# Taking out the landing waits inside the second expert layer's token scatter

## The reference, cut to what matters

```python
logits = flat.astype(jnp.float32) @ router_w.T + router_bias
scores = jax.nn.softmax(logits, axis=-1)
topk_scores, topk_idx = jax.lax.top_k(scores, TOPK)
topk_scores = topk_scores / jnp.clip(topk_scores.sum(axis=-1, keepdims=True), 1e-12, None)
h = jax.nn.silu(jnp.einsum('nd,ehd->neh', flat, gate_w)) * jnp.einsum('nd,ehd->neh', flat, up_w)
expert_out = jnp.einsum('neh,edh->ned', h, down_w)
sel = jnp.take_along_axis(expert_out, topk_idx[:, :, None], axis=1)
out = (sel * topk_scores.astype(flat.dtype)[:, :, None]).sum(axis=1)
out = out + jax.nn.silu(flat @ sgate_w.T) * (flat @ sup_w.T) @ sdown_w.T
```

## Time and profile before

| | |
|---|---|
| three runs | 1621.0, 1626.23, 1638.97 us; median 1626.23 us |
| the profiled execution | 1626.23 us, its span 1624.5 us, so 1.7 us lie around it |
| PE busy | 1368.0 us (84% of the span) |
| DVE, ACT, POOL busy | 774.4 us, 438.9 us, 295.9 us |
| scatters of stage 7 | 1265.4 to 1368.6 us in the span |

### The profile page before, as it was taken

How to read it: one execution, slowest core, us unless ns; L and a number is a source line. 1 busy time by engine, 2 the same in 40 slices (tenths; PEclk the granted TensorE clock), 3 DMA queues, 4 the chain that set the end, 5 groups by cost and what they waited for, 6 DMA issues and landing times.

```text
span 1624.5 us, 18832 instructions
## 1 busy us (share of the span) xinstructions
PE 1368.0 (84%) x6042; PEld 767.9 (47%) x6043; DVE 774.4 (48%) x2121; ACT 438.9 (27%) x840; POOL 295.9 (18%) x310
## 2 busy tenths in 40 slices
PE   5999999999934779999998829999957689898983
PEld 3434334333413434444443525666645445677862
DVE  7282383275277435545565422222256563344546
ACT  2122122222105224544353302333222211232320
POOL 2010010010011100000000030111111454145560
PEclk9899999999977769999998859999976579999997
DMA  9999990000001000000000391111024622244436
GB/s 313 338 336 327 335 315 5 0 0 0 0 5 48 1 1 1 1 1 1 1 29 1 108 358 33 33 33 33 23 75 156 232 85 95 82 135 152 144 122 261
DMA packets 136659, 171.35 MB, mean 105 GB/s; under 512 B 8464, under 2 KB 124944, under 8 KB 136464
## 3 DMA queue, kind: packets, MB, share of 16 engines
q1 hardware_dynamic: 126992, 143.81, 28.6%
q0 software_dynamic: 9600, 26.65, 4.5%
HBM read 68.11 MB, written 102.32 MB: 105 GB/s over the span
## 4 chain that ended last, share of the span: by engine, by line
PE 69%; DVE 15%; issue 5%; ACT 4%; SPq 4%; DMA 2%; another core or an unknown queue 1%; POOL 0%; DVEq 0%; ACTq 0%; POOLq 0%
PE psum L1819 16%; PE psum L1204 5%; PE psum L1188 5%; PE psum L1987 5%; PE psum L992 4%; PE psum L880 3%; PE psum L2043 3%; PE psum L1009 2%; PE psum L1776 2%; DVE arena L2558 2%; PE psum L2020 2%; PE psum L1973 2%; PE psum L2067 2%; PE psum L890 2%; SPq L2664 2%
## 5 line engine op out<-in xcount | busy, mean ns | idle before, releaser
L1819 PE MATMUL psum<-arena 128*128 128x512 f32 (+1 forms) x576 | 291.8, 635 | 0.3
L1819 PEld LDWEIGHTS psum<-arena 128*128 128x128 f32 (+1 forms) x576 | 96.5, 192 | 162.8 <-issue 160.0
L2558 DVE TENSOR_REDUCE arena<-psum 128x4 f32<-128x616 f32 x128 | 102.1, 797 | 126.9 <-PE psum L1987 125.6
L1987 PE MATMUL psum<-arena 32*128 32x308 f32 x512 | 112.0, 516 | 24.2 <-DVE arena L2558 22.9
L1132 POOL DMA_INDIRECT ys<-xnT,arena x96 | 92.2, 961 | 122.4 <-DVE xnT L1098 97.5
L2153 ACT ACTIVATE arena<-psum,arena 128x512 f32<-128x512 f32 x72 | 49.1, 686 | 234.2 <-PE psum L1819 222.2
L2267 ACT ACTIVATE arena<-psum 128x2048 f32<-128x2048 f32 x40 | 75.0, 1875 | 76.8 <-PE psum L2024 59.8
L992 PE MATMUL psum<-arena,xn 128*128 x384 | 89.9, 388 | 2.0 <-ACT xn L1043 0.9
L1204 PE MATMUL psum<-arena,xn 128*128 x384 | 88.6, 385 | 2.0 <-ACT xn L1250 2.0
L1188 PE MATMUL psum<-arena,side 128*128 x192 | 88.1, 602 | 1.0 <-ACT side L1243 0.6
L1987 PEld LDWEIGHTS psum<-arena 32*128 32x128 f32 x512 | 41.9, 200 | 92.1 <-DVE arena L2558 61.3
(11 more groups left out here) (391 smaller groups left out, 2220.3 us busy)
## 6 DMA issues: line engine op xcount, KB each, us to landing
xs<-zeros SPq DMA_DIRECT2D x8, 8576.0 KB, 59.8
arena<-in_W SPq DMA_DIRECT2D x16, 1024.0 KB
xn<-xs SPq DMA_DIRECT2D x96, 134.0 KB
arena<-in_gate_up SPq DMA_DIRECT2D x4, 2048.0 KB
arena<-ys SPq DMA_DIRECT2D x4, 2048.0 KB, 15.0
arena<-in_down SPq DMA_DIRECT2D x4, 1024.0 KB
xs<-zeros SPq DMA_DIRECT2D x1, 3120.0 KB, 17.0
side<-xs SPq DMA_DIRECT2D x24, 130.0 KB
```

The lines of the kernel that those rows point to most:

```text
L1819: ins = pe.matmul(bank[dict(hn=4, r=5, z=6, xn=7)[k]][:], lhs[:, cols], r, start=(start and n == 0), stop=(stop and n == len(w) - 1))
L1987: ins = pe.matmul(bank[4 + i][:, 0:2 * M].rearrange("p (h m) -> p h m", h=2), qhT[rows, n % 3, c, t * P:(t + 1) * P], keys[rows, l, c, b, ...
L2558: dve.tensor_reduce(neg[:, n % 2, t, 2 * pair:2 * pair + 2, 2 * c:2 * c + 2], psum[:, 4:6, 0:2 * M].rearrange("p b (h m) -> p b h m", h=2) ...
```

## The change

The wait of L870 and L871 is deleted. Before, POOL held back after the first, second and third tile of each group until every scatter started so far had landed; now it starts the 16 scatters of a group one behind another. The wait for `slots_ready` at the start of each group stays, and so does SP's wait for all 64. Everything behind in the file moves up by two lines.

```diff
@@ -867,8 +867,6 @@
                 for k in range(K4):
                     pool.indirect_dma_start(xs7, bass.IndirectOffsetOnAxis(r7["slot_i"][:, n, k:k + 1].bitcast(U32), 0),
                                             xn[:, g, t], None).then_inc(scattered.sem, 16)
-                if t < GT - 1:
-                    pool.wait_ge(*scattered.at(7, 16 * K4 * (n + 1)))
 
```

## The result

| | before | after |
|---|---|---|
| median | 1626.49 us (20 runs) | 1650.28 us (20 runs) |
| range of the runs | 1617.84 to 1641.11 | 1639.44 to 1668.39 |
| the profiled execution | 1626.23 us, span 1624.5 | 1653.95 us, span 1652.2 |

The changed kernel takes 1.0126 times as long, with a 95% interval of 1.0097 to 1.0155: some 20 us more where no change was forecast. The time lies outside the range.

The account below looks back on a forecast made before the run. PE, with 69% of the chain, was taken to bound the kernel, POOL holding 0%. POOL's 22.4 us and SP's 9.9 us stay hidden, so 1626.23 + 0 = 1626.2 us, range 1616 to 1638.

Parts of the forecast that it names:

- POOL's side: POOL's scatter issue: 22.4 us of waits go, 12.3 us of new waits for DVE's L701 come, last issue ends 9.9 us earlier.
- PE's step into the first quad: PE passing from L890 to L985: still without idle time, near 1391.5 as before, 0 us gained.
- SP's wait at the last weights: SP after its eight token loads: waiting for PE grows from 3.2 to 13.1 us, last weights still at 1382.37.
- POOL's gain: Removed scatter waits: 22.4 us less on POOL, 9.9 us less up to SP, 0 us on PE.
- Two costs have to be asked for, since the same scatters now stand denser: DMA queue and DVE speed beside denser scatters: DMA 0 to some us inside the 9.9, taken as 0; DVE 0.
- The term of the sum that was put at zero: The change's effect on the whole time: 0 us, the 9.9 us hidden by PE's products L880 and L890.
- all it did before that was the shared expert, which takes nothing from the scatters: PE before L985: its work doesn't depend on the scatters, so it arrives at 1391.48 as before.
- Stage 5 shows this very case: Stage 5's 16 scatters without waits, beside transfers filling the DMA engines to 0.97: 961 ns an issue, nothing piled up.
- L697 and L931 at their usual durations: DVE instructions beside scatters and without: 419 to 420 and 686 to 689 ns, so engines don't slow each other by 1%.
- 0 on both sides: Cost of DVE and POOL working beside each other: bounded at 0 us.
- The jam: POOL's 64 starts: its queue fills and starts slow; 1675.5 us if all went at 2.51 us a scatter; chance 0.03.
- What would show it: Trace signs: starts end near 1358.7, L948 near 1361.2, L985 near 1391.5; PE pausing or issues well over 1.0 us refute.

Follow-up runs that it names:

- e6_eights: Changed kernel with landing waits put back after the second and fourth tile of each group, at most eight starts in a row: 1633.00 us, 1.0015.
- e11_twelve: Changed kernel with landing waits put back after the third and fourth tile of each group, runs of twelve and four: 1635.06 us, 1.0023.
- e14_rows: Changed kernel with each indirect scatter sent to 128 consecutive rows, the experts' part of the result left out: 1641.85 us, one run.
- e3_half: Changed kernel with one landing wait put back in each group, after its second tile: 1636.01 us, 1.0054.

## Why the prediction was wrong, point by point

**What held.** POOL's side came as worked out: the pace of 1.27 us, 20.0 us for a group, twelve waits gone, waits for L701 in their place. PE's step into the first quad has no idle time in front of it, and SP's wait at the last weights grew from 3.2 us, to 18.7 where 13 were expected. POOL's gain was off the path, as forecast: no kernel that keeps the scatters and has fewer waits came out faster than before.

**What failed: "Two costs have to be asked for, since the same scatters now stand denser".** There the prediction asked for the DMA engines' load and for DVE's speed beside POOL, took both as 0, and both are 0: 110 GB/s flowed in the densest run, and a start kept to 956 to 983 ns. (The 57 on POOL that it divides by are 56 scatters and an IOTA, and instead of some ten scatters in the queue beside the weights there were four or five; neither matters.) The third cost was not asked for: how long a finished product takes to be known by the engine that waits for it. That went from 0.04 us to as much as 8.1 us, and added 2.31, 2.37, 7.59 and 8.52 us to the four steps. The term of the sum that was put at zero is 20.8 us in the profiled execution and 1.26% of the time over all runs. PE came to L985 (now L983) late because its own work was held up, where the prediction had it unchanged since "all it did before that was the shared expert, which takes nothing from the scatters".

**The precedent that misled: "Stage 5 shows this very case".** It has the same 16 starts at the same pace, but in that stretch PE, DVE and ACT are busy 0.00 us. Nothing on other engines could be seen waiting, so it could show that no transfer piles up, but not that nobody else suffers. And before the change no run beside working engines was longer than four, save where one group's last tile ran into the next group's first: eight, which costs nothing measurable in e6_eights. The trace of before held no row for this case, and the prediction should have priced it as unknown.

**L697 and L931 at their usual durations** prove that an instruction runs at its speed once started. They can't show a late start; the bound "0 on both sides" was read from the wrong column. The gap between a releaser's end and the waiter's start is the one to read.

**The rivals.** The jam was the only one with a mechanism on the right side, and its mechanism is wrong: POOL kept its pace and wasn't held. SP was indeed released too late for PE, but since all of PE's own work had come late. The clearest miss of "What would show it" is that every sign of a jam it named was absent while the time rose by 20 us. Its last sentence, that everything from L985 on keeps its old place, is what fell.

**What stays open.** Shown are the conditions under which it happens: indirect starts, about 1.3 us apart, more than eight in a row, with PE's signals to DVE and ACT late by up to 10.6 us. The rivals are out: the semaphore, the landings, the addresses and the length of POOL's run each by a kernel, the number in flight by the packets, which are two at a time before and after, save beside the weights in group 0. What the starts and the signals share was not found. A picture that fits most of it, only argued: each indirect start leaves some work behind that takes between 1.3 and 1.6 us somewhere on the way of the signals; at 1.27 us apart it piles up, and signals wait behind it. For it speaks that no late signal was found in the first ten microseconds of a run that had a rest before it, that the delay goes on for 1.2 to 3.0 us behind a run's end, and that it carried over a break of 1.76 us. Against it speaks that it isn't regular: two products that ended 12.0 us into a run were on time (group 1 of e11_twelve, the first run of e14_rows), one 18 us into e3_half's first border too, and in the changed kernel itself a signal of 1316.24 got through after 1.0 us and one of 1345.01 only after 8.1. That groups 0 and 1 lose less than 2 and 3 was not followed up.

One more trace of it is in the profiles. Each scatter raises its semaphore 16 times, 1024 times in all, and of these the trace has recorded 267 in the changed kernel, 584 before, 934 at the even pace of 1.58 us, but 1024 of 1024 and 2048 of 2048 for the plain transfers. The increments all arrived, since SP waits for their full number. So what the profiler records of raised semaphores gets lost where indirect starts stand dense, even in runs that do no harm: 584 are those of fours and eights before, and e6_eights, with no late logits, has 371. That is a hint at the path of the increments and no proof of a cause.

No version beats the kernel before. The medians of runs of eight, of the pauses without waits and of the even pace all lie within 0.3% of it, none below.

## What to carry to other kernels

A wait that looks like waste on an engine off the path can be a brake that others live on, so a trace in which it is in force can't price its removal; look for the resource that it keeps free, and take a precedent only from a stretch in which the other engines were at work. After such a change read, for each waiter, the gap between its releaser's end and its start: "remote" lines that were not there before point to signals and not to work. Where indirect transfers stand in a row beside other engines' work, keep to runs of eight or spread them to 1.6 us apiece, which here cost nothing measurable.

## What the hardware showed that was not expected

- Indirect transfers started by POOL every 1.27 us, twelve or more in a row, can delay PE's signals to DVE and ACT by 1 to 10.6 us (the logits' by up to 7.4, 8.1 and 9.85 us in three kernels), while the scatters keep to 956 to 983 ns, the bytes flow at 108 GB/s and each scatter is through 2.05 to 2.12 us after its start.
- The same at 1.58 us apart, or in runs of at most eight, costs nothing that could be measured (1.0029 and 1.0015, both intervals around 1).
- 32 plain transfers in a row, 0.53 us apart, with twice the landings, delay nothing (0.04 us in all groups).
- Spreading the landings over four semaphores doesn't help (1.0130), nor does a wait for an older scatter that makes no pause (1.0135).
- The trace records 267 of the 1024 increments of dense indirect scatters, 934 at 1.58 us apart, and all of those of plain transfers.
- Once PE waited for the late signals, the granted clock was 0.68 in 1350 to 1360 where it had been 1.00.
